# A Mamba mixer with a mixture of experts: dt as one rounded product over 96 rows, TensorE's order around up, and experts marked by match-replace in the first stage

## The reference

```python
xn = layernorm(x)
# Mamba mixer: 1024 channels, 16 states, rank 32
x_, gate = split(xn @ in_proj_w.T); xc = silu(causal_conv4(x_) + conv_b)
ts, B, C = split(xc @ x_proj_w.T, [32, 48])
dt = softplus(ts @ dt_proj_w.T + dt_proj_b)
state_t = state_{t-1} * exp(dt_t * A) + dt_t * B_t * xc_t
y_t = sum_s(state_t * C_t) + xc_t * D
mixer = (y * silu(gate)) @ out_proj_w.T
# experts: 64, top 6 of each token, 64 slots each; a shared expert beside them
scores = softmax(xn @ gate_w.T); top 6 -> slots -> silu(x@w_gate) * (x@w_up) @ w_down
shared = silu(xn @ sw_gate) * (xn @ sw_up) @ sw_down
```

## Time and profile before

| | us |
|---|---|
| median of 3 runs | 1353.33 (1353.22 to 1354.02) |
| the profiled execution | 1353.8 |
| its span, first to last instruction | 1351.9 |
| stage 1 | 0 to 264 |
| the 32 steps | 264 to about 1048 |
| stage 3 | to 1352 |
| busy over the span: PE, DVE, ACT, POOL | 1278.2, 1096.0, 903.6, 867.6 |
| weight loads on PE (overlapping) | 800.7 |
| mean granted TensorE clock | 0.984 |

### The profile page before, as it was taken

How to read it: one execution, slowest core, us unless ns; L and a number is a source line. 1 busy time by engine, 2 the same in 40 slices (tenths; PEclk the granted TensorE clock), 3 DMA queues, 4 the chain that set the end, 5 groups by cost and what they waited for, 6 DMA issues and landing times.

```text
span 1351.9 us, 53063 instructions
## 1 busy us (share of the span) xinstructions
PE 1278.2 (95%) x21591; PEld 800.7 (59%) x21591; DVE 1096.0 (81%) x1260; ACT 903.6 (67%) x1920; POOL 867.6 (64%) x456
## 2 busy tenths in 40 slices
PE   6898989599999999999999999999999899999998
PEld 4666767355555545555455555455555578787876
DVE  5798989779999989999989999889999464655554
ACT  4655666478788878888878888678787243434343
POOL 3445348268998979989879898978998330303030
PEclk9999999789999999999999999999999899999999
DMA  7252544869999999999989999989898753122130
GB/s 288 101 229 104 215 152 163 265 176 306 265 312 274 308 276 252 312 285 290 302 238 311 293 274 313 280 263 310 246 313 285 231 198 123 65 83 104 52 134 31
DMA packets 129762, 304.86 MB, mean 226 GB/s; under 512 B 18560, under 2 KB 20352, under 8 KB 127872
## 3 DMA queue, kind: packets, MB, share of 16 engines
q1 hardware_dynamic: 122096, 285.13, 64.0%
q0 software_dynamic: 7600, 18.91, 7.3%
HBM read 213.91 MB, written 56.77 MB: 200 GB/s over the span
## 4 chain that ended last, share of the span: by engine, by line
PE 56%; DVE 12%; issue 7%; ACT 4%; DVEq 1%; DMA 1%; ACTq 0%; PEldq 0%; POOLq 0%
PE p_dBx L1315 15%; DVE state L1004 8%; PE p_dBx L1374 7%; PE p_y L1324 7%; PE p_g L1301 6%; PE p_g L1284 4%; PE p_dt L1264 3%; PE p_y L1385 3%; ACT dA L1154 2%; PE p_g L1385 2%; PE p_u L1385 2%; PE p_dt L1385 2%; PE p_u L1270 2%; DVE out_operand_parts L1039 1%; PE p_u L1284 1%
## 5 line engine op out<-in xcount | busy, mean ns | idle before, releaser
L1004 DVE TENSOR_TENSOR_SCAN state<-dA,state_carry,p_dBx 128x512 f32<-128x512 f32 x512 | 626.6, 1266 | 76.2 <-PE p_dBx L1315 72.3
L940 POOL TENSOR_TENSOR h_times_C<-state,C_bcast 128x1024 f32<-128x1024 f32 x128 | 315.8, 2467 | 60.4 <-DVE state L1004 59.6
L940 POOL TENSOR_TENSOR C_bcast<-state,C_bcast 128x1024 f32<-128x1024 f32 x128 | 318.6, 2764 | 28.9 <-DVE state L1004 28.3
L1315 PEld LDWEIGHTS p_dBx<-B_diagonals,step_rows 64*32 64x32 f32 x16384 | 236.4, 106 | 150.7 <-issue 148.6
L1315 PE MATMUL p_dBx<-B_diagonals,step_rows 64*32 64x128 f32 x16384 | 311.3, 276 | 11.8 <-DVE state L1004 7.4
L1154 ACT ACTIVATE dA<-dt_blocks_odd,A_par 128x512 f32<-128x512 f32 x256 | 169.6, 710 | 23.4 <-DMA dt_blocks_odd<-step_rows 23.4
L1154 ACT ACTIVATE dA<-dt_blocks_even,A_par 128x512 f32<-128x512 f32 x256 | 169.6, 710 | 12.2 <-DMA dt_blocks_even<-step_rows 12.2
L280 POOL TENSOR_TENSOR w_in_parts_lo<-C_bcast,w_in_parts_hi 128x512 fp32r<-128x512 f32 x64 | 89.9, 1407 | 106.6 <-ACT w_in_parts_hi L493 106.2
L954 POOL TENSOR_TENSOR step_rows<-step_rows 128x512 f32<-128x512 f32 x16 | 22.2, 1416 | 182.2 <-DMA step_rows<-moe 182.2
L371 DVE SCALAR_TENSOR_TENSOR conv_out<-conv_in,conv_w,conv_out 128x512 f32<-128x512 f32 x96 | 96.1, 1011 | 7.4 <-ACT conv_out L515 5.1
L1284 PE MATMUL p_u<-w_up_pair,step_rows 128*64 128x352 f32 x512 | 92.5, 480 | 2.7 <-issue 2.7
(11 more groups left out here) (185 smaller groups left out, 2086.2 us busy)
## 6 DMA issues: line engine op xcount, KB each, us to landing
w_gate_pair<-in_w_gate SPq DMA_DIRECT2D x32, 1408.0 KB
w_up_pair<-in_w_up SPq DMA_DIRECT2D x32, 1408.0 KB, 7.9
...
dt_blocks_odd<-step_rows SPq DMA_DIRECT2D x256, 64.0 KB
...
```

The lines of the kernel that those rows point to most:

```text
L940: pool.tensor_tensor(hc[m][:, b, :, :], hb[:, q, :, :], Cb[:, NM * (c % 2) + GS * m:NM * (c % 2) + GS * m + GS, :], ALU.mult).then_inc(s_h ...
L1004: ins = dve.tensor_tensor_scan(hb[:, g % NBUF, s, :], dA[:, g % NBUF, s, :], pB[:, g % 2, :].rearrange("p (t s) -> p s t", s=GS)[:, s, :], ...
L1315: ins = pe.matmul(out[DB * p:DB * p + DB, half, j, :, :], dtxT[k, j * P + DB * b:j * P + DB * b + DB], diag[k, ND * cp + 2 * j + p // 2, a ...
```

## The change

Three parts that meet in one list for each engine.

1. dt. ScalarE and VectorE make the rounded parts of w_dt once (96 rows: hi, lo, hi; stored as `wdt_d`), ScalarE and GpSimd the parts of ts for each chunk, stored by six DMAs into `ts_d` (hi, hi, lo). dt is then one float32r product over 96 rows. ts is loaded once a chunk (every eighth step) and not for each step.
2. TensorE in a step: dBx 4 and `dtx_T` ahead of up, up in one piece. The gating (`gate`) goes from group 3 to group 4 on VectorE.
3. Stage 1: VectorE's match-replace of the top six marks the experts, in place of indices and compares; the ranks are turned at n = 8 and searched in their own chunk; the layer norm stands earlier; `x_lo` goes from GpSimd to VectorE; ScalarE's second copy of the tokens (`take_xT_hi`) stands after two silus of gates; the list transposes follow the last x_proj; the first gather stands at the end of GpSimd's list of stage 1.

```diff
-DT_AT, GATE_AT, HH_AT = 1, 3, 5
+DT_AT, GATE_AT, HH_AT = 1, 4, 5
-        RSTD_AT, RANKS_TURN, X_TURN, SEARCHES, PER_CHUNK = 12, 12, 12, CAP // 16, (T // P) // (NCH - 1)
+        RSTD_AT, RANKS_TURN, X_TURN, SEARCHES, PER_CHUNK = 9, 8, 12, CAP // 16, (T // P) // (NCH - 1)
+            sp.dma_start(wdt_raw, io["w_dt"]).then_inc(s_wraw, 16)
...
+            def store_ts(c):
+                sp.wait_ge(s_tslo, c + 1)
+                for h in range(2):
+                    own, r = slice(h * CH // 2, (h + 1) * CH // 2), slice(E * h, E * h + RANK)
+                    for n, part in enumerate((ts_hi[c], ts_hi[c], ts_lo[c])):
+                        sp.dma_start(io["ts_d"][c][n * RANK:(n + 1) * RANK, own], part[r, :].bitcast(F32)).then_inc(s_tss, 16)
...
+                if c > 0:
+                    store_ts(c - 1)
                 if c == NCH - 1:
                     tile_in.load_gate(sp, 0)
...
+            store_ts(NCH - 1)
+            sp.wait_ge(s_tss, 96 * NCH)
...
+            ts_los(NCH - 1)
             pool.wait_ge(s_zd, 16 * (1 + 2 * T // P))
             for a in range(2):
                 pool.dma_start(io["moe"][a * ROWS + T:(a + 1) * ROWS, :], io["moe"][a * ROWS:a * ROWS + CAP, :]).then_inc(keep["s_sc"], 16)
                 pool.wait_ge(keep["s_sc"], 16 * a + 16)
+            pool.wait_ge(s_xns, 16 * NCH)
+            pool.wait_ge(s_idx, 1)
+            pool.indirect_dma_start(zero[:, :], None, io["xn_d"],
+                                    bass.IndirectOffsetOnAxis(ap=gidx[:, 0:1].bitcast(U32), axis=0)).then_inc(keep["s_xg"], 16)
...
+                chain(dve.memset(m8[:, :, TOPK:], -1.0))
+                settled()
                 for j in range(TJ):
-                    chain(dve.max_index(ix[:, j, :], m8[:, j, :], xs[:, j, H:XS]))
+                    chain(dve.match_replace(marked[:, j, :], m8[:, j, :], xs[:, j, H:XS], -2.0))
                 settled()
+                dve.scalar_tensor_tensor(val[:, :, :], marked[:, :, :], 0.0,
+                                         tio[:, c * TJ:c * TJ + TJ].unsqueeze(2).to_broadcast([P, TJ, E]),
+                                         ALU.is_lt, ALU.mult).then_inc(s_val, 1)
...
+                search(c, 0)
+                search(c, 1)
+                if c < NCH - 1:
+                    x_lo(c + 1)
+                search(c, 2)
+                search(c, 3)
...
                     dBx(i, cp, 3)
+                    dBx(i, cp, 4)
+                    dtx_T(i + 1)
                     pe.wait_ge(s_hT, i + 1)
                     pe.wait_ge(s_wu, 16 * i + 16)
-                    gate_or_up(pU, wu, range(KH // 2), s_ups)
-                    dBx(i, cp, 4)
-                    gate_or_up(pU, wu, range(KH // 2, KH), s_ups)
-                    dtx_T(i + 1)
+                    gate_or_up(pU, wu, range(KH), s_ups)
                     dBx(i, cp, 5)
...
-        self.wdt = sb("w_dt", [RANK, P])
-        self.ts = sb("ts_tile", [RANK, CH])
+        self.wdt = ctx.enter_context(nc.sbuf_tensor("w_dt_parts", [R3, P], F32R))
+        self.ts = ctx.enter_context(nc.sbuf_tensor("ts_parts", [R3, CH], F32R))
...
+        sp.dma_start(self.wdt[:, :].bitcast(F32), self.io["wdt_d"][:, i % ND, :]).then_inc(self.s_wdt, 16)
+        if i % ND == 0:
+            sp.dma_start(self.ts[:, :].bitcast(F32), self.io["ts_d"][i // ND]).then_inc(self.s_wdt, 16)
```

More of the change, by code:

```diff
@@ L97, in stage1 @@
         m8 = sb("top8", [P, TJ, 8])
-        ix = sb("top8_index", [P, TJ, 8], U32)
-        ixf = sb("top8_index_f", [P, TJ, 8])
-        with ExitStack() as own:
-            eioi = own.enter_context(nc.sbuf_tensor("expert_iota_i", [P, TJ, E], I32))
-        chosen = sb("chosen", [P, TJ, E])
-        eio = sb("expert_iota", [P, TJ, E])
+        marked = sh
         tioi = sb("token_rank_i", [P, NCH * TJ], I32)
@@ L113, in stage1 @@
         lst = sb("slot_rank", [E, CAP])
-        lt1 = sb("slot_tmp1", [E, CAP])
-        lt2 = sb("slot_tmp2", [E, CAP])
-        lidx = sb("slot_token", [E, CAP])
-        lid2 = sb("slot_token_pairs", [NP, 2 * CAP])
-        lid2s = sb("slot_token_sums", [NP, 2 * CAP])
+        lt1, lt2, lidx = (sh[0:E, n, :] for n in range(3))
+        lid2, lid2s = (lT[0:NP, n * 2 * CAP:(n + 1) * 2 * CAP] for n in range(2))
         xr = sb("conv_in", [P, ND, CH + TAPS - 1])
         xt = sb("conv_out", [P, ND, CH])
-        zero = sb("zeros", [P, XS])
+        zero = keep["xg"]
         sz = sb("silu_gate", [P, 2, CH])
@@ L129, in stage1 @@
         pV = pS[0:E, :]
-        pL_gather = pIn[0][:, 0:NP]
-        pL_scatter = pIn[1][:, 0:NP]
+        pL_gather, pL_scatter = (pS[:, n * NP:n * NP + NP] for n in range(2))
         s_x, s_w = sem("x_loaded"), sem("weights_loaded")
@@ L280, in w_lo @@
                 pool.tensor_tensor(wp[1][:, n % 2, :], win[:, tile, :], wp[0][:, n % 2, :], ALU.subtract).then_inc(s_wlo, 1)
-            def x_lo(c):
-                pool.wait_ge(s_xhi, c + 1)
-                pool.tensor_tensor(xp[1][:, c % 2, :, :], xnT[:, :, :], xp[0][:, c % 2, :, :], ALU.subtract).then_inc(s_xlo, 1)
             def first_diagonals(k):
@@ L302, in first_dt, with ts_los @@
                                    tile_in.xa[:, 0, :].rearrange(by_row, i=2, j=JD), ALU.mult).then_inc(s_dt0, 1)
+            def ts_los(c):
+                pool.wait_ge(s_ssm, c + 1)
+                pool.wait_ge(s_tshi, c + 1)
+                pool.tensor_tensor(ts_lo[c], ssm[:, :], ts_hi[c], ALU.subtract).then_inc(s_tslo, 1)
             rstds(0)
@@ L310, in _ @@
                     w_lo(c, n)
+                    if c > 0 and n == 2:
+                        ts_los(c - 1)
                     if c < NCH - 1 and n == RSTD_AT:
@@ L434, in _ @@
             for c in range(NCH):
-                last = c == NCH - 1
-                if c > 0:
-                    for part in range(SEARCHES):
-                        search(c - 1, part)
                 conv(c, 0)
@@ L443, in _ @@
                 scores(c)
[L444 to L445 removed]
+                if c == 0:
+                    w_dt_lo()
                 conv(c, 3)
+                if c < NCH - 1:
+                    ln_stats(c + 1)
                 conv(c, 4)
[L448 to L449 removed]
+                conv(c, 5)
+                if c < NCH - 1:
                     ln_norm(c + 1)
[L451 to L453 removed]
                 conv(c, 6)
[L455 to L458 removed]
                 conv(c, 7)
[L460 to L462 removed]
+                search(c, 0)
+                search(c, 1)
+                if c < NCH - 1:
+                    x_lo(c + 1)
+                search(c, 2)
+                search(c, 3)
             settled()
@@ L744, in stages2and3 @@
         carry = sb("state_carry", [P, ND + STEPS, NS])
-        xg = sb("tokens_of_pair", [P, XS])
-        sg = sb("sigmoid_g", [P, I])
-        hh = sb("expert_h", [P, I])
+        xg = keep["xg"]
+        sg, hh = (rows2[:, n, 0:I] for n in (4, 5))
         wsc = sb("score_of_slot", [P, STEPS + 2])
@@ L755, in stages2and3 @@
         s_wd = sem("w_down_loaded")
-        s_xg = sem("tokens_gathered")
+        s_xg = keep["s_xg"]
         s_si = sem("scatter_rows_set")
@@ L926, in scatter @@
                                         yo[:, n % 2, :], None, compute_op=ALU.add).then_inc(s_sc, 16)
-            gather(0)
             for t in (hh[:, :], wsc[:, :], sz):
```

110 lines of the change are left out of this document (53 added, 57 removed).

## The result

| | before | changed |
|---|---|---|
| median (us) | 1353.28, 4 runs (1352.8 to 1354.02) | 1334.03, 4 runs (1330.7 to 1337.05) |
| ratio | | 0.9846, 95% interval 0.982 to 0.9872 |
| span of the profiled execution | 1351.9 | 1335.2 |
| first down of the steps starts | 295.2 | 285.9 |
| 31 periods (down to down), first to last down | 752.8 | 750.8 |

The change made the kernel 19 us faster. The forecast was 38, so half of it came. Starts of down are the first rows of down in TensorE's timeline (as 684.74 in the earlier trace rows); from them the 16.7 us between the two spans are 9.26 up to the first down, 1.99 in the 31 periods, 4.08 in the stretch behind them and 1.37 in what follows.

The account below looks back on a forecast made before the run. TensorE's list was taken to bound a step, its waits a chunk's saving. 12.9 (chunks 0 to 2) + 0.4 (end of stage 1) + 24.8 (steps) = 38.1 off gave a median of 1315; forecast 1310 to 1320, range 1301 to 1333.

Parts of the forecast that it names:

- What bounds the kernel: In the steps: a step is as long as TensorE's list, busy 98%, 23.63 us from down to down.
- dt and the clean step: In a step: 0.82 from dt and 0.28 from dBx 6, less a 0.16 wait, leaves 0.94 us saved.
- The saving of dt: On TensorE in a step: the new product of 96 rows takes 0.23 in place of 1.05, 0.82 us less.
- The wait for x times D: Ahead of the sums in a step: TensorE arrives 1.10 earlier against a cover of 0.94, a wait of 0.16 us.
- The allowance for the round, and for more DMA share: In the steps: 0.15 us off 0.94 for dt's round through SP's 16 block copies and DMA share rising to 0.97.
- Rival (b): In the steps: dt's round through ScalarE, VectorE and SP's block copies holds the step; 1337 to 1340 us, chance 0.13.
- Chunks 0 to 2: In stage 1: TensorE's waits in a chunk go, 4.3 us each, 12.9 for three.
- The end of stage 1: Last chunk to the first steps: gains 2.6, 0.8 and 0.7 less 3.7 of SP's stores, 0.4 us in sum.
- GpSimd's copies: At the end of stage 1: two copies of zeros start near 254, end near 264, so the gather stands where it stood.
- The 1.55 put down for the second dt: At the end of stage 1, at the low clock: 2.07 x 3/4 = 1.55 us saved, 0.7 over what the steps counted.
- SP's tail: After the last x_proj: six stores of ts in place of two, 2.5, behind a copy and subtraction, 1.2; 3.7 us lost.
- The same 0.8: In the steps: 0.94 less 0.15, taken as 0.8 us saved in each of 31 steps, 24.8 in all.

Follow-up runs that it names:

- experiment 4's second run: The changed kernel without the loads of w_gate in the steps and with the load of x ahead of w_up: 1314.94 us.
- experiment 2: Three edits of the changed kernel: product of dt issued four times, 1343.13 us; TensorE's old order with gate at group 3, 1329.33; both together, 1343.87.
- experiments 1 and 2: The changed kernel measured again, unedited, 1334.20 us; and its edits with product of dt issued four times, TensorE's old order, or both (1343.13, 1329.33, 1343.87).
- stage 1 alone: The changed kernel with TensorE's old order, gate at group 3, and the product of dt issued four times: 1343.87 us, ratio 0.9926.
- experiments 3 and 4: Their two edits together on the changed kernel, loads of w_gate left out of the steps and load of x ahead of w_up: 1314.94 us.
- the kernel before without the loads: The kernel before the change with the loads of w_gate left out of the steps: 1349.14 us, ratio 0.9955.
- experiment 3: Loads of w_gate left out of the steps, in the changed kernel, 1316.01 us, and in the kernel before, 1349.14 us.
- Experiment 6: The changed kernel with the last six stores of ts issued ahead of the load of w_up and the waits for earlier stores: 1330.67 us.

## Why the prediction was wrong in its size, step by step

**What bounds the kernel.** Right. TensorE's list set the steps: with the product at its old price and the old order they are back near the old period (23.75 in the mean of the first chunks' steps, 23.84 before, the three long ones left out).

**dt and the clean step.** Right to 0.04: forecast 23.63 - 0.94 = 22.69, measured 22.73 where no transfer is late (the median of experiment 4's second run). The saving of dt was 0.63 from its own start and 0.81 with the transposes ahead of it, where 0.82 was forecast. The wait for x times D came as foreseen, but at 0.59 in place of 0.16: x times D is done 19.74 behind the down, as before (19.75), and TensorE would reach the sums 1.49 sooner and not 1.10. Against the kernel before, TensorE's rows from gate to the transposes of h, and from there to the sums, take some 0.2 less each, for which no term stood in the sum. So 1.49 - 0.59 = 0.90 where 1.10 - 0.16 = 0.94 was forecast: the total is closer than its two parts, which is luck in part.

**The allowance for the round, and for more DMA share: the step that failed.** "I take 0.15 off for that": this term was mis-sized. Product and order together measured 1343.9 - 1334.2 = 9.7 in experiment 2, where 24.8 + 0.7 = 25.5 had been put down. The missing 15.8 are 0.51 a step, so the allowance had to be 0.66 and not 0.15; in the first profile, with 2.0 in place of 24.8, it was 0.9. The profiles of experiments 1 and 2 say where it is missing: against stage 1 alone the changed kernel gains 11.5 in the first 23 periods (543.9 against 555.4), for which 18.4 had been put down, and 4.1 from there to the down behind the steps (215.1 against 219.2), for which 6.4 had.

For the first 23 periods the cause is shown. With the two reliefs of experiments 3 and 4 ScalarE waits 0.4 us for blocks and VectorE none for x, and these periods are 0.94 a step shorter than before, the forecast's figure ahead of its allowance. What late landings had taken from them is 0.94 less the 0.50 a step that they gained with all loads. For the last chunk it is not shown: there the same kernel, its late transfers gone, takes 196.3 in eight periods, and the kernel before without the loads 193.2. And the 33 of experiment 3 is near the forecast's 38 without being made of its terms: in the two profiles, 35.3 apart, 13.9 lie ahead of the first down, 14.9 in the first 23 periods and 6.5 behind them.

Rival (b) was the right mechanism, but not in all steps: it holds some, and lets others through at 22.7. The prediction read that TensorE's rows stood end to start and took it for room in the queues. The view that would have said more is the wait of 1.71 in the earlier trace rows: ScalarE already waited 35.6 us for blocks before the change, hidden behind TensorE's list.

**Chunks 0 to 2.** Right: forecast 55.1 a chunk, measured 54.57 and 54.56; all five waits of the earlier trace rows gone. x_lo took 2.36 on VectorE, four match-replaces 0.21 each:

```profile
93.84 0.21 DVE L410 MATCH_REPLACE8 logit_shift<-top,xn_scores 128x64 f32<-128x64 f32 x1
...
124.50 2.36 DVE L420 TENSOR_TENSOR xT_parts_lo<-dt_blocks_even,xT_parts_hi 128x2048 fp32r<-128x2048 f32 x1
```

By **the Trainium skill**, VectorE: DVE Perf Modes, The TRN2 errata, x_lo would be 2.29; the row has 2.36, within 3% of it. By the ends of x_proj chunk 0 gave 3.6, chunks 1 and 2 gave 4.8 and 4.9 where 4.3 was forecast for each, and the last one 2.1 in place of 2.6: 15.4 in all against 15.5.

**The end of stage 1.** Wrong in two terms of opposite sign. GpSimd's copies had been set at 254, the time of the old trace, without taking off what the chunks had gained; they started at 242.25, and the gather came 13 us sooner. With it TensorE was busy sooner and its clock back sooner, and the first step is 5.5 shorter. The 1.55 put down for the second dt is not in it, since four products in place of one move the first down by 0.04. And SP's tail was put down at 3.7; it gave back 11.6 of 15.4, because SP's list, at whose end the barrier stands, now is the longest. Experiment 6 shows 3.45 of it. That stage 1 alone measured 11.8, and the forecast without its dt terms also was 12.9 + 2.6 - 3.7 = 11.8, is luck: these errors cancelled.

**The last chunk of steps.** Not foreseen: x_parts behind the gate. The same 0.8 was carried to all 31 steps, but where VectorE's extra work stands in the same group the new order lost 4 us in eight periods. The stretch behind the 32nd down gave the 4 back, so the time shows little of it. That stretch is 24.4 before and 23.5 with stage 1 alone, both with the old order, and 20.4 and 20.3 in the changed kernel: it belongs to the order and not to stage 1.

**Left open.** Why the same program takes 12 us more or less in its steps from run to run; why the last chunk does not gain when no transfer is late; whether fewer bytes or a shorter transfer ahead would free the blocks; and the mixed version, the new order in the first three chunks and the old in the last, which was not tried.
